# First cross-attention of a decoder layer: context split sooner, all turned blocks copied by VectorE, repeated products on TensorE, low halves of two row tiles sooner

## The chip, the cores and the metric

The kernel runs on 1 core of one Trainium2 chip. The metric is the device time of one execution in microseconds (us); lower is better. The inputs are float32 and the whole layer is one launch.

## The reference

One pre-norm decoder layer without a norm scale: self-attention, cross-attention to a context, and a gated feed-forward part with low-rank experts. Shapes: `x` is (32, 100, 512), the context (32, 361, 128), of which the causal mask lets only the first 100 rows count.

```python
def _L0_xattn_ref(q, latent_kv, Wq, Wkv_expand, Wout):
    B, S, H, NH, L = (2, 512, 512, 16, 128)
    HD = H // NH
    qp = q @ Wq.T
    kv = latent_kv @ Wkv_expand.T
    k, v = jnp.split(kv, 2, axis=-1)
    # qh, kh, vh: (b, NH, s, HD)
    scores = jnp.einsum('bhqd,bhkd->bhqk', qh, kh) * inv_sqrt_d
    causal = jnp.tril(jnp.ones((sq, sk), dtype=bool))
    scores = jnp.where(causal, scores, jnp.finfo(scores.dtype).min)
    attn = jax.nn.softmax(scores, axis=-1)
    out = jnp.einsum('bhqk,bhkd->bhqd', attn, vh)
    return out @ Wout.T

x = x + _L0_attn_ref(_layernorm(x), ...)     # 16 heads of 128, RMS-normed q and k
x = x + _L0_xattn_ref(_layernorm(x), ctx_512, ...)   # 16 heads of 32
x = x + _L0_ffn_ref(_layernorm(x), ...)      # 1408 wide, 8 experts, 2 chosen
```

## The kernel before

The layer runs in two phases. **Phase A** is self-attention over all 32 batches, in 128 steps `n` (4 groups of 4 heads by 32 batches, `STEPS` = 128). Each engine has its own loop over `n` and goes ahead by semaphores alone: in step `n` TensorE makes the scores of step `n+1`, projects what later steps need, and mixes the values of step `n-1`; ScalarE takes the exponentials of `n+1`; VectorE takes maxima, sums and low halves. Products are made in three float16 matrix multiplications (high by high, high by low, low by high; `three`, lines 1561 to 1563), so most tensors are split into a high half by ScalarE and a low half by VectorE.

**Phase B** handles the batches in groups of 5 (500 rows in 4 tiles of 125), group 0 first: cross-attention, then the feed-forward part. From group 1 on, each cross-attention is interleaved with the last product of the group before (`some_out`: three multiplications per piece, into bank 7 of the eight PSUM banks). Group 0 has no group before it (`last_nb` is 0), so nothing is interleaved there.

The start of group 0 is woven into the last steps of phase A by `begin_cross(n)` on each engine: at `B_KEYS` (126) ScalarE and VectorE split the context (`context_hi`, `context_lo`), TensorE turns two row tiles and projects three of the four key chunks (`keys`); at 127 the fourth; at 128 the values, at 129 the queries. TensorE runs `begin_cross(126)` ahead of the mixing of step 125. Weight pieces of phase B are loaded by SyncE one step ahead and split in phase A as well; the last of those (piece 13, at step 126) is split by ScalarE at line 817 and by VectorE at line 1107, each in program order with the rest of its step.

Then `cross_attention(0, 5, 0)` loops over `b` = 0 to 5. In round `b` TensorE writes the causal mask (L1832, 4 multiplications, each after the exponentials that last read its bank) and adds the scores of batch `b` (L1838, 32 small ones), turns the four probability blocks `i` of batch `b-1` (L1854, 4 each, into banks 4 and 5 in turn, after GpSimd normalized them), and mixes the values of batch `b-1` (`mix`, L1810). Somebody must copy the four turned blocks out of PSUM first: ScalarE copies 0 and 3 (L973), VectorE 1 and 2 (L1368). ScalarE takes the exponentials of batch `b`, 16 instructions of one head each (L982), VectorE the maxima before them (L1359) and the reciprocals of the sums after them (L1380); `split_b_hi` and `split_b_lo` split the last three weight pieces beside it. `mix` waits on two counters, `pTe` and `pTd`.

After round 5, VectorE adds the output projection to the rows (`add_residual`, L1384 and the statistics behind it), normalizes them (`norm`, L1227), TensorE turns the rows (`turn_row`, L1654), ScalarE takes their high halves (`row_hi`, L886) and VectorE the low halves (`row_lo`, L1232). Three of the four row tiles are "early": `route` (L1561 to 1563 with 8 columns) and `factors` for these run before the fourth tile's.

## Time and profile before

| what | value |
|---|---|
| median of 3 runs | 2577.39 us (2575.33 to 2578.66) |
| the profiled execution | 2567.62 us |
| its span | 2565.8 us |
| TensorE busy | 2458.2 us, 96% |
| VectorE, ScalarE, GpSimd busy | 1553.2, 1339.9, 843.8 us |
| mean granted TensorE clock | 0.982 of full |

The span runs from the first to the last instruction of the profiled execution; that execution's own time is 1.8 us longer than its span. PE is TensorE, DVE VectorE, ACT ScalarE, POOL GpSimd, SP SyncE. PEclk is the share of the full TensorE clock (2.4 GHz) that was granted, so 0.50 is 1.2 GHz. Phase B's first group begins near 1249 us of the span (turning of the first rows), its cross-attention loop at 1287 us, and its feed-forward part at 1367 us.

### The profile page before, as it was taken

How to read it: one execution, taken by the hardware profiler on the slowest of the kernel's cores; microseconds unless marked ns; L12 is line 12 of the kernel's file. 1: busy time of each engine (PE TensorE's matmuls, PEld its weight loads, DVE VectorE, ACT ScalarE, POOL GpSimd, SP SyncE). 2: the span in 40 equal slices, each digit the busy share in tenths (PEclk: the TensorE clock that was granted, in tenths of full speed). 3: DMA queues.
4: the chain of work that ended last, by engine and by line, in shares of the span. 5: the costliest groups of instructions: out<-in, count | busy, mean ns of one | idle time of the engine just before them, and what ended most of it. 6: DMA issues, size and time to landing. Idle time of an engine off the chain costs nothing.

```text
span 2565.8 us, 47726 instructions
## 1 busy us (share of the span) xinstructions
PE 2458.2 (96%) x16474; PEld 1333.3 (52%) x16474; DVE 1553.2 (61%) x3592; ACT 1339.9 (52%) x4109; POOL 843.8 (33%) x794
## 2 busy tenths in 40 slices
PE   6998999999999999999889999999999999999998
PEld 3554555554555555444454465465465465465466
DVE  7786766666666666666555745644645645655644
ACT  4554555555555555555454554554554563564533
POOL 3333333333333333333222422422422422422412
PEclk9999999999999999999979999999999999999999
DMA  6786667777677767797611001001001001001000
GB/s 157 149 180 161 152 151 162 167 161 169 138 170 162 168 144 190 157 195 171 139 59 57 30 13 53 5 14 54 1 18 54 1 18 54 1 18 41 7 17 14
DMA packets 456281, 241.79 MB, mean 94 GB/s; under 512 B 389136, under 2 KB 391824, under 8 KB 455284
## 3 DMA queue, kind: packets, MB, share of 16 engines
q1 hardware_dynamic: 456034, 238.63, 39.8%
q8 instruction: 139, 2.28, 0.4%
q14 instruction: 108, 0.88, 0.1%
HBM read 78.66 MB, written 32.77 MB: 43 GB/s over the span
## 4 chain that ended last, share of the span: by engine, by line
PE 89%; DVE 4%; ACT 3%; issue 3%; POOL 1%; DVEq 0%; POOLq 0%; ACTq 0%
PE ps L1561 24%; PE ps L1562 24%; PE ps L1563 24%; PE ps L1740 3%; PE ps L1741 2%; PE ps L1742 2%; PE ps L1854 2%; ACT mem L982 2%; PE ps L1838 1%; PE ps L1810 1%; PE ps L1750 1%; PE ps L1754 1%; PE ps L1752 1%; PE ps L1832 1%; PE ps L1579 1%
## 5 line engine op out<-in xcount | busy, mean ns | idle before, releaser
L1561 PE MATMUL ps<-mem 128*128 128x512 f16 (+7 forms) x3992 | 1227.9, 326 | 47.7 <-issue 31.4
L1562 PE MATMUL ps<-mem 128*128 128x512 f16 (+7 forms) x3992 | 1239.5, 326 | 0.0
L1563 PE MATMUL ps<-mem 128*128 128x512 f16 (+7 forms) x3992 | 1223.0, 325 | 0.0
L1561 PEld LDWEIGHTS ps<-mem 128*128 128x128 f16 (+3 forms) x3992 | 413.6, 104 | 374.6 <-issue 52.8
L1563 PEld LDWEIGHTS ps<-mem 128*128 128x128 f16 (+3 forms) x3992 | 414.7, 104 | 316.5 <-issue 8.6
L1562 PEld LDWEIGHTS ps<-mem 128*128 128x128 f16 (+3 forms) x3992 | 416.4, 104 | 304.8 <-issue 8.0
L757 POOL TENSOR_TENSOR mem<-mem 128x500 f32<-128x500 f32 (+1 forms) x231 | 268.7, 1164 | 470.3 <-ACT mem L1058 289.7
L707 POOL TENSOR_TENSOR mem<-mem 128x8 f32<-128x8 f32 x100 | 163.7, 1637 | 507.4 <-DVE mem L1145 507.4
L852 ACT ACTIVATE mem<-ps,mem 100x100 f32<-100x100 f32 x512 | 169.1, 346 | 186.4 <-DVE mem L1175 185.5
L1513 DVE TENSOR_TENSOR mem<-mem 128x500 f16<-128x500 f32 (+1 forms) x231 | 144.5, 649 | 171.3 <-ACT mem L1040 167.4
L719 POOL TENSOR_TENSOR mem<-mem 100x400 f16<-100x400 f32 x128 | 158.7, 1239 | 182.7 <-ACT mem L862 182.7
L832 ACT ACTIVATE mem<-ps 128x512 f32<-128x512 f32 x200 | 117.7, 589 | 168.8 <-DVE mem L1139 86.1
L771 POOL TENSOR_TENSOR mem<-mem 100x400 f32<-100x400 f32 x128 | 107.5, 852 | 290.5 <-DVE mem L1380 290.4
L1040 ACT ACTIVATE mem<-mem 128x500 f16<-128x500 f32 (+1 forms) x231 | 127.9, 585 | 111.7 <-POOL mem L757 111.3
L1206 DVE SCALAR_TENSOR_TENSOR mem<-ps,mem 128x512 f32<-128x512 f32 x100 | 69.0, 690 | 174.7 <-PE ps L1563 174.6
L982 ACT ACTIVATE mem<-ps,mem 100x100 f32<-100x100 f32 x512 | 168.5, 379 | 8.2 <-DVE mem L1359 8.2
L842 ACT ACTIVATE mem<-ps,mem 128x128 f16<-128x128 f32 x400 | 113.9, 368 | 83.7 <-POOL mem L707 83.7
L1139 DVE TENSOR_REDUCE mem<-mem 128x4 f32<-128x512 f32 x200 | 136.2, 681 | 31.8 <-ACT mem L832 31.8
L1524 DVE TENSOR_TENSOR mem<-ps,mem 128x500 f32<-128x500 f32 (+1 forms) x154 | 97.3, 632 | 66.9 <-PE ps L1563 66.6
L713 POOL TENSOR_TENSOR mem<-mem 100x400 f32<-100x400 f32 x128 | 109.1, 852 | 73.0 <-DVE mem L1185 73.0
L1153 DVE SCALAR_TENSOR_TENSOR mem<-ps,mem 128x128 f32<-128x128 f32 x400 | 112.1, 343 | 34.3 <-POOL mem L707 34.2
L982 ACT ACTIVATION_READ_ACCUMULATOR mem<-ps,mem 100x1 f32 x512 | 124.9, 244 | 0.0
(123 smaller groups left out, 3043.9 us busy)
## 6 DMA issues: line engine op xcount, KB each, us to landing
x<-mem SPq DMA_DIRECT2D x100, 256.0 KB, 2.8
mem<-x SPq DMA_DIRECT2D x75, 256.0 KB, 3.6
mem<-in_x SPq DMA_DIRECT2D x50, 256.0 KB, 3.5
mem<-x SPq DMA_DIRECT2D x12, 1000.0 KB
mem<-mem SPq DMA_DIRECT2D x32, 200.0 KB
mem<-mem SPq DMA_DIRECT2D x6, 1000.0 KB
out<-mem SPq DMA_DIRECT2D x6, 1000.0 KB
mem<-in_wq SPq DMA_DIRECT2D x16, 256.0 KB, 4.2
```

Source lines behind the costliest of these rows:

```text
L707: pool.tensor_tensor(rr[:, u % 2, :], ms[:, u % 2, :], half[:, 0:2 * HG], ALU.pow).then_inc(s["rr"], 1)
L719: pool.tensor_tensor(p_split[0:S, n % 2, 1, :, 0:S], probs[0:S, :, :], p_split[0:S, n % 2, 0, :, 0:S], ALU.subtract).then_inc(s["plo"], 1)
L757: pool.tensor_tensor(hh[:, i, 0:gs], gate[:, i, 0:gs], ub[:, 0:gs] if i == 0 else up[:, i - 1, 0:gs], ALU.mult).then_inc(c["h"], 1)
L832: act.activation(sq[:, :, :], bank(kind, u).rearrange("p (h d) -> p h d", d=D), ACT.Square).then_inc(s["sq" + kind], 1)
L852: op = act.activation(probs[0:S, h, :], ps_s[0:S, h * S:(h + 1) * S], ACT.Exp, bias=mx[0:S, h:h + 1], accum_out=den[0:S, h:h + 1])
L982: op = act.activation(cprobs[0:S, i, m, :], ps[0:S, i, m * S:(m + 1) * S], ACT.Exp, bias=cmx[0:S, i, m:m + 1], accum_out=cden[0:S, i, m:m ...
L1040: act.activation(hb_hi[:, jj, 0:gs] if i == 0 else hs_hi[:, i - 1, 0:gs], hh[:, i, 0:gs], ACT.Copy).then_inc(c["hhi"], 1)
L1139: dve.tensor_reduce(ss[:, i, m * HG:(m + 1) * HG], sq[:, :, :], AX.X, ALU.add).then_inc(s["ss"], 1)
L1513: dve.tensor_tensor(lo, hh[:, i, 0:gs], hi, ALU.subtract).then_inc(c["hlo"], 1)
L1561: pe.matmul(out_ap, ah, bh, start=(i == 0), stop=False)
L1562: pe.matmul(out_ap, ah, bl, start=False, stop=False)
L1563: mm = pe.matmul(out_ap, al, bh, start=False, stop=(i == len(pairs) - 1))
```

## The change

Four edits, all for group 0 alone.

1. The context is split one step sooner: `context_hi` and `context_lo` move from step 126 to step 125 (`B_CONTEXT`). ScalarE now waits there for the last transposing DMA of self-attention (`qkT`), whose space the split context takes. On ScalarE the two `row_hi` of step 126 move ahead of that step's exponentials, on VectorE the two `row_lo` ahead of that step's `inverse_sum`.
2. VectorE copies all four turned blocks in rounds 1 to 4; ScalarE still copies 0 and 3 in round 5. The copies stand between VectorE's maxima and reciprocals, and the low half of a weight piece goes behind the reciprocals.
3. TensorE repeats products of 512 columns (`repeat`) into bank 7, which nobody reads: 2 ahead of each of three mask blocks, 2 ahead of turning block 2, 4 ahead of `mix`.
4. After round 5, `row_lo` of tiles 0 and 1 stands ahead of `add_residual` of tile 3.

```diff
+        B_CONTEXT = STEPS - 3
 # ScalarE
             def begin_cross(n):
+                if n == B_CONTEXT:
+                    act.wait_ge(s["qlo"], ALL)
+                    act.wait_ge(s[f"qkT{(ALL - 1) % 2}"], turned(ALL - 1))
+                    context_hi(0, GS)
                 if n == B_KEYS:
-                    act.wait_ge(s["qlo"], ALL)
-                    context_hi(0, GS)
                     for t in range(2):
                         row_hi(0, t, TM, t)
...
                 for u in turned_tile(n):
                     rows_hi(u)
+                if n <= B_KEYS:
+                    begin_cross(n)
                 if 0 <= n + 1 < STEPS:
                     exponentials(n + 1)
...
-                if n == B_KEYS:
-                    begin_cross(n)
...
                 for b in range(nb + 1):
-                    if b:
+                    if b and (last_nb or b == nb):
                         take_turned(b - 1, 0)
                     if b < nb:
                         exponentials(b, 0)
                         exponentials(b, 1)
-                    if b:
+                    if b and (last_nb or b == nb):
                         take_turned(b - 1, 3)
 # VectorE
                 if n == B_KEYS:
-                    context_lo(0, GS)
-                    for t in range(2):
-                        row_lo(0, t, TM, t)
                     for m in range(3):
                         take_ck(0, GS, m)
...
                     take_o_lo(n - 2)
+                if n == B_CONTEXT:
+                    context_lo(0, GS)
+                if n == B_KEYS:
+                    for t in range(2):
+                        row_lo(0, t, TM, t)
...
-                                    ).then_inc(c["pTd"], 1)
+                                    ).then_inc(c["pTe" if i in (0, 3) else "pTd"], 1)
...
                         for i in range(4):
                             largest_scores(b, i)
-                            if b and i >= 2:
+                            if b and i and not last_nb:
+                                take_turned(b - 1, i - 1)
+                            if b and i >= 2 and last_nb:
                                 take_turned(b - 1, i - 1)
...
+                        for i in range(4):
+                            invert_sum(b, i)
+                            if b and i == 0 and not last_nb:
+                                take_turned(b - 1, 3)
                         for n in (beside_first(b - 1) if b and not last_nb else []):
                             split_b_lo(n)
-                        for i in range(4):
-                            invert_sum(b, i)
...
+                ahead = 0 if last_nb else 2
+                for t in range(ahead):
+                    row_lo(g * 2 * NT + nt, t, tm, t)
                 for t in range(len(early), nt):
                     add_residual(t)
                 first = len(early) if not last_nb else min(2, len(early))
-                for t in range(first):
+                for t in range(ahead, first):
                     row_lo(g * 2 * NT + nt, t, tm, t)
 # TensorE
+                def repeat(n):
+
+                    for _ in range(0 if last_nb else n):
+                        pe.matmul(ps[:, 7, :], cwo_hi[:, 0, 0:P], cwo_hi[:, 1, :], start=True, stop=True)
...
                             if b:
+                                if i:
+                                    repeat(2)
                                 pe.wait_ge(c["exp"], g * 4 * GB + 4 * (b - 1) + i + 1)
...
                         if b:
+                            if b < nb and i == 2:
+                                repeat(2)
                             pe.wait_ge(c["norm"], g * 4 * GB + 4 * (b - 1) + i + 1)
...
                     if b:
+                        if b < nb:
+                            repeat(4)
                         mix(b)
```

ScalarE at steps 125 and 126 of self-attention, before. L852 are the exponentials, L897 is `context_hi`, L886 `row_hi`, L817 the high half of weight piece 13, L879 `take_o_hi`.

```order
L852 ACTIVATE mem<-ps,mem 100x100 x4
L869 ACTIVATE mem<-ps 128x512
L862 ACTIVATE mem<-mem 100x4x100
L879 ACTIVATE mem<-ps 128x4x100
L852 ACTIVATE mem<-ps,mem 100x100 x4
L862 ACTIVATE mem<-mem 100x4x100
L897 ACTIVATE mem<-mem 128x500
L886 ACTIVATE mem<-ps 128x4x125 x2
L817 ACTIVATE mem<-mem 128x1408
L879 ACTIVATE mem<-ps 128x4x100
```

The same stretch after the change, in which the lines are L853, L898, L887, L818 and L880.

```order
L898 ACTIVATE mem<-mem 128x500
L853 ACTIVATE mem<-ps,mem 100x100 x4
L870 ACTIVATE mem<-ps 128x512
L863 ACTIVATE mem<-mem 100x4x100
L880 ACTIVATE mem<-ps 128x4x100
L887 ACTIVATE mem<-ps 128x4x125 x2
L853 ACTIVATE mem<-ps,mem 100x100 x4
L863 ACTIVATE mem<-mem 100x4x100
L818 ACTIVATE mem<-mem 128x1408
L880 ACTIVATE mem<-ps 128x4x100
```

The split of the context and of the rows went ahead of exponentials; the weight piece stays ahead of the `take_o_hi` that follows it.

VectorE in round 1 of the cross-attention loop, before (L1359 maxima, L1368 copies of turned blocks, L1107 a weight piece, L1380 reciprocals, L1351 `take_o`).

```order
L1359 TENSOR_REDUCE mem<-ps 100x4 x3
L1368 COPY mem<-ps 100x400
L1359 TENSOR_REDUCE mem<-ps 100x4
L1368 COPY mem<-ps 100x400
L1107 SCALAR_TENSOR_TENSOR mem<-mem 128x1408
L1380 RECIPROCAL mem<-mem 100x4 x4
L1351 TENSOR_TENSOR mem<-ps,mem 128x4x100
```

After (L1364 maxima, L1373 copies, L1385 reciprocals, L1110 the weight piece, L1356 `take_o`).

```order
L1364 TENSOR_REDUCE mem<-ps 100x4 x2
L1373 COPY mem<-ps 100x400
L1364 TENSOR_REDUCE mem<-ps 100x4
L1373 COPY mem<-ps 100x400
L1364 TENSOR_REDUCE mem<-ps 100x4
L1373 COPY mem<-ps 100x400
L1385 RECIPROCAL mem<-mem 100x4
L1373 COPY mem<-ps 100x400
L1385 RECIPROCAL mem<-mem 100x4 x3
L1110 SCALAR_TENSOR_TENSOR mem<-mem 128x1408
L1356 TENSOR_TENSOR mem<-ps,mem 128x4x100
```

Two copies more, one of them between the second and third maximum, and the weight piece behind all reciprocals.

TensorE from the turning of a round to the scores of the next, before (L1854 turning, L1810 `mix`, L1832 masks, L1838 scores).

```order
L1854 MATMUL ps<-mem 100x100 x16
L1810 MATMUL ps<-mem 32x100 x16
L1832 MATMUL ps<-mem 100x400 x4
L1838 MATMUL ps<-mem 100x100 x16
```

After (L1875, L1827, L1851, L1857; L1815 is `repeat`).

```order
L1875 MATMUL ps<-mem 100x100 x8
L1815 MATMUL ps<-mem 128x512 x2
L1875 MATMUL ps<-mem 100x100 x8
L1815 MATMUL ps<-mem 128x512 x4
L1827 MATMUL ps<-mem 32x100 x16
L1851 MATMUL ps<-mem 100x400
L1815 MATMUL ps<-mem 128x512 x2
L1851 MATMUL ps<-mem 100x400
L1815 MATMUL ps<-mem 128x512 x2
L1851 MATMUL ps<-mem 100x400
L1815 MATMUL ps<-mem 128x512 x2
L1851 MATMUL ps<-mem 100x400
L1857 MATMUL ps<-mem 100x100 x16
```

Twelve repeated products stand in each such stretch; the first one (scores of batch 0 to those of batch 1) has only the six among the masks.

## Rows read from the trace of the kernel before

**Rows 1.** Busy us (x instructions) per engine by stretch; last: granted clock, DMA share, GB/s.

```profile
1256.00:1259.50 3.50, 3.44 (x9) 1.34 (x10) 2.50 (x4) 1.38 (x1) 0.00 (x0) 0.50 0.45 120
1297.00:1315.50 18.50, 15.87 (x173) 11.29 (x169) 11.15 (x24) 15.64 (x73) 6.65 (x8) 0.50 0.35 109
1351.80:1358.50 6.70, 6.68 (x46) 5.22 (x47) 0.42 (x1) 0.00 (x0) 0.00 (x0) 0.50 0.32 131
1494.00:1534.00 40.00, 39.99 (x427) 27.73 (x426) 22.57 (x59) 26.96 (x142) 14.36 (x18) 1.00 0.01 2
...
1554.00:1554.50 0.50, 0.50 (x3) 0.15 (x1) 0.43 (x3) 0.00 (x0) 0.00 (x0) 0.50 1.04 303
```

**Rows 2.** Timeline of TensorE around the first keys: start, us, what, idle before.

```profile
1248.95 1.03 PE L1654 MATMUL ps<-mem 125*128 125x125 f32 x8
1256.06 0.58 PE L1561 MATMUL ps<-mem 128*128 128x500 f16 x1 [6.08 <-issue]
...
1264.37 0.20 PE L1561 MATMUL ps<-mem 100*128 100x100 f16 x1
```

**Rows 3.** Timeline of ScalarE in the same stretch.

```profile
1246.50 0.35 ACT L852 ACTIVATE mem<-ps,mem 100x100 f32<-100x100 f32 x1 [2.39 <-DVE mem L1175]
...
1257.24 1.38 ACT L817 ACTIVATE mem<-mem 128x1408 f16<-128x1408 f32 x1 [1.38 <-DMA mem<-in_wu]
```

**Rows 4.** Timeline of VectorE in the same stretch.

```profile
1254.95 1.01 DVE L1248 SCALAR_TENSOR_TENSOR mem<-mem 128x500 f16<-128x500 f32 x1 [2.04 <-ACT mem L897]
...
1260.52 1.62 DVE L1107 SCALAR_TENSOR_TENSOR mem<-mem 128x1408 f16<-128x1408 f32 x1
1263.05 0.69 DVE L1206 SCALAR_TENSOR_TENSOR mem<-ps,mem 128x512 f32<-128x512 f32 x1 [0.92 <-PE ps L1563]
1263.66 0.56 DVE L1190 SCALAR_TENSOR_TENSOR mem<-ps,mem 128x400 f16<-128x400 f32 x1
```

**Rows 5.** Chain of waits: exponentials of batch 0, and round 2 of the loop.

```profile
1289.55 5.34 ACT mem L982 x32
...
1306.33 0.85 PE ps L1854 x4
...
1310.77 1.56 PE ps L1810 x32
1312.33 1.62 PE ps L1832 x4
1313.95 1.60 PE ps L1838 x32
```

**Rows 6.** Timeline of TensorE, group 1's loop: the same steps at full clock.

```profile
1499.84 0.38 PE L1742 MATMUL ps<-mem 128*125 128x512 f16 x1
1500.05 0.84 PE L1832 MATMUL ps<-mem 100*100 100x400 bf16 x4
1500.82 0.96 PE L1838 MATMUL ps<-mem 32*100 32x100 f32 x32
...
1501.72 0.47 PE L1854 MATMUL ps<-mem 100*100 100x100 f32 x3
```

**Rows 7.** Timeline of VectorE, group 0, round 2: maxima, then one copy.

```profile
1306.35 1.54 DVE L1359 TENSOR_REDUCE mem<-ps 100x4 f32<-100x400 f32 x3
1307.87 0.57 DVE L1368 COPY mem<-ps 100x400 f32<-100x400 f32 x1
```

**Rows 8.** Timeline of TensorE: turning in round 4, output projection of tiles 0 and 1.

```profile
1324.70 3.21 PE L1854 MATMUL ps<-mem 100*100 100x100 f32 x16
...
1332.07 0.63 PE L1561 MATMUL ps<-mem 128*125 128x512 f16 x1
...
1335.99 0.51 PE L1854 MATMUL ps<-mem 100*100 100x100 f32 x4
```

**Rows 9.** Timeline behind the loop: low halves, first `route` product.

```profile
1349.93 1.84 DVE L1232 TENSOR_TENSOR mem<-ps,mem 128x500 f16<-128x500 f32 x3
...
1351.82 0.27 PE L1561 MATMUL ps<-mem 128*125 128x8 f16 x1 [3.25 <-DVE mem L1232]
```

## The prediction

> **What bounds the kernel now.** I read the shares of busy time first: TensorE is busy 96% of the span, so time can only be won where it waits or runs at half clock. The busy time and granted clock by stretch show where: the change touches group 0 alone, and there the cross-attention loop runs at a clock of 0.50 from 1297.0 to 1315.5, while the same loop of group 1, with multiplications of 512 columns between its parts, runs at 1.00 [rows 1]. TensorE's timeline then shows three places in group 0 that end in waits: 6.08 us idle before the first keys [rows 2], the rounds of the loop, and 3.25 us idle before `route` [rows 9]. The chain of waits says what a round is made of [rows 5].
>
> **Head: the context sooner.** At 1249.98 TensorE has turned its two row tiles and stands until 1256.06. What ends last is VectorE's `context_lo` (1254.95 plus 1.01), behind ScalarE's `context_hi` [rows 2, 4]. One step earlier ScalarE waits 2.39 us for a maximum anyway [rows 3], and the new wait on the transposing DMA is one that the scores of step 126 have too, so `context_hi` costs nothing there; `context_lo` falls into a wait of VectorE on those exponentials. If it did not, its 1.01 us would delay the reciprocals. The keys can then start at about 1250.0, and the two `row_hi` put ahead of the last exponentials delay them by no more than their own 1 us, on a path that has 4.9 us to spare (below).
>
> Not all 6 us are won, since the next wait stands close behind. The mixing of step 126 (1264.37 [rows 2]) needs the output of step 125 copied and split. On ScalarE that copy stands behind weight piece 13, which starts when its DMA lands, at 1257.24, and that DMA is not moved [rows 3]. So ScalarE is free near 1258.5 and has copied at 1259.0; VectorE, from 1258.7, does its half of the piece (1.62), a sum (0.69), and the low half (0.56) [rows 4]: 1258.7 + 2.87 = 1261.5. TensorE gets through the keys, a mixing, an output projection, the fourth keys and two turned tiles by about 1256.6 and stands for 4.9 us. The gain is 1264.4 - 1261.5 = 2.9 us. From it goes the clock: after 6.08 us idle TensorE ran its next 3.4 us at 0.50 [rows 1], a loss of 1.7 that lies inside the 14.4 us compared. After 4.9 us idle I expect half clock again, now behind the mixing, and take 1.2 of the 1.7, as part of the slow time may lie in the idle time. **Head: 1.7 us**, from 0.2 (the piece's DMA lands a little later, full loss) to 2.9.
>
> **The loop.** Before, the third round starts turning at 1306.33 and the fifth at 1324.70 [rows 5, 8]: 9.2 us a round. The chain in it [rows 5]: first turned block 0.85, ScalarE's copy, two sets of exponentials (16 take 5.34, so 8 take 2.7), its other copy, `mix` 1.56, masks 1.62, scores 1.60; what is left of 9.2 for the two copies is 0.9. `mix` waits for ScalarE's second copy, and all TensorE's parts are at half clock.
>
> After, I count from the end of the scores, at full clock. Masks cost 0.77 there and scores 0.90 (starts in group 1 [rows 6]); a turned block is 0.35 (group 1, half of 0.85 and a bit less), `mix` 0.82, half of 1.56 and a bit. A repeated product takes 0.215, as one of 512 columns from start to start there [rows 6]; half clock doubles it. VectorE: a maximum each 0.49, a copy each 0.49 with 0.57 to its end [rows 7]. It runs maximum 0 to 0.55, 1 to 1.0, copy 0 to 1.6, maximum 2 to 2.0, copy 1 to 2.6, maximum 3 to 3.0, copy 2 to 3.5, a reciprocal, copy 3 to 4.2. TensorE turns blocks 0 and 1 by 0.7, repeats two (1.1), turns 2 at 1.6 and 3 at 2.6 behind the copies that free their banks, repeats four (3.8), waits until 4.2 and mixes until 5.0. ScalarE, now without copies, has its four sets of exponentials done at 0.65 + 5.15 = 5.8. Masks with six repeated products: 5.0 + 0.77 + 1.3 = 7.06, past the last exponentials at 5.8; scores to **8.0 us**. So the repeated products themselves now bound the round; VectorE is close behind, since its weight piece (1.6) and `take_o` (0.57) come after the last reciprocal: 5.9 + 2.1 = 8.0. ScalarE ends near 7.5. Group 1's rounds, with 18 such products, also take 8.0.
>
> That gives 3 rounds at 9.2 - 8.0 = 3.6 us. The first stretch (batch 0 to batch 1) is bound by exponentials either way and wins only the clock of its last mask and the scores, 0.2 + 0.65 = 0.85. The last: output projection of tile 0 started 7.4 after the scores (1332.07 against 1324.70 [rows 8]) and can start once the exponentials end, 5.85, so 1.5; its 12 products took 3.9 us of which half lay at half clock, against 2.6 [rows 8], 1.3 more. Sum 7.3. The clock may still fall: in the first stretch TensorE stands for a maximum and the first exponentials, 2 us, and then has short pieces between exponentials. I take off 1.0 for that, an estimate between nothing and about 2 (one stretch of 3.4 us at half, as in the head). **Loop: 6.3 us.**
>
> Moved with it: piece 16's DMA is issued only after the low half of piece 14, now 3 us later in its round; ScalarE needs it after the next exponentials, one round of 8 later, and I count at most 0.5 us, within the rounding.
>
> **Tail.** `route` waits for three low halves in a row (1.84 [rows 9]) behind the fourth tile's statistics. Two of them now run during the projection: the wait shrinks by 2 x 0.6 = 1.2 us, to some 2.0. TensorE then ran 6.7 us at 0.50 [rows 1], worth 3.3 us. Part may come back. But in group 1 the clock was also 0.50 just after `route` with no idle at all before it [rows 1], so 8-column products do not hold the clock here. I take 1.0, between 0 and 3.2. **Tail: 2.2 us.**
>
> **Sum.** 1.7 + 6.3 + 2.2 = 10.2 us. Against the profiled execution's 2567.62 that is 2557.4; against the median, 9.8 above it, 2577.4 - 10.2 = **2567.2 us**. About 0.2% (5.2 us) is what a measurement of this kernel can tell from no change. All of TensorE's work behind the tail is dense, so nothing gives the time back.
>
> **Rivals.**
>
> *A. The clock swings.* The twelve products leave three gaps of about 0.5 us in a round, and the first stretch has longer ones. For it: the clock was 0.50 there with TensorE busy 15.87 of 18.5 us [rows 1], so being busy alone did not raise it. Against it: group 1 holds 1.00, but with 18 products and no gaps. If every round spends one stretch of about 3 us at half, it costs 1.2 to 1.7 more; the loop gains 2 and the whole is 6: 2571.5. The Trainium skill, TensorE: Matmul & The Clock Gate, section A second HAM failure mode: psum-queue depth-cycling, speaks for this rival: small idles between groups of matmuls, it says, let the clock go back and forth. By that rule the loop comes out as in this rival; no row here shows a loop with such gaps and such products.
>
> *B. Slower: repeated products at half clock.* If they don't raise the clock, each is 0.43 us, and they stand on TensorE's own path: turning and the first two 2.56, the rest of the turning 4.25, four more 5.96, `mix` 7.5, masks with six more 11.7, scores 13.3 us a round. Three rounds lose 4.0 each and the last 1.4: 13.4, less head and tail 3.9, 9.5 slower: 2587. It decides from where more than about two of the rounds stay at half. Against it: the first keys, dense products of 500 columns, brought the clock up within 3.5 us [rows 1], and at half clock the rounds would be dense.
>
> *C. VectorE takes over.* It makes two copies more a round, holds back maxima 2 and 3, and has its weight piece behind the last reciprocal. If its order costs 1 us a round, rounds are 9.0: the loop wins 3.3 and the whole about 7 or, with a late piece 16, 3: 2573. The sum above is nearly tied, which speaks for it; group 1, where VectorE has no pieces, says nothing.
>
> *D. More than forecast.* Full clock kept in head, loop and tail: 2.9 + 7.3 + 4.4 = 14.6: 2562.8.
>
> **Numbers.** Forecast 0.50, A 0.20, B 0.05, C 0.10, D 0.15. The range 2561.5 to 2573.5 takes in D, A and C with a run's own spread, and leaves out B and the far end of C. Faster by over 0.2% (below 2572.2): forecast, D, most of A: 0.84. Same: C and the rest of A: 0.11. Slower: B, 0.05.
>
> **What would show it.** In the profile after: keys at about 1250 with no idle ahead; a wait of some 5 us now ahead of the mixing of step 126, behind ScalarE's weight piece at 1257; rounds of 8.0 us with a granted clock near 1.00 and no copy on ScalarE in them; output projection 5.9 us after the last scores; two low halves ahead of the fourth tile's sum and a wait of about 2 us before `route`. A clock of 0.5 to 0.7 in the rounds says A, a round over 11 us says B, a TensorE waiting for VectorE's first maximum or copy with a clock of 1.00 says C. I would be wrong in kind if the loop gained nothing at full clock.

## The result, and the profile after

The changed kernel takes 2570.52 us (median of 20 runs, 2561.25 to 2574.64). The kernel before, run beside it, takes 2574.78 us (20 runs, 2564.77 to 2579.11). The ratio is 0.9984 with a 95% interval of 0.9977 to 0.9992: 4.1 us faster, between 2.1 and 5.9. The forecast was a gain of 10.2 us.

The profiled execution took 2572.42 us, its span 2570.6 us. Its first 1256 us (self-attention) are 7.1 us longer than in the profile before; five more profiles with the same code there have it at 1248.3 to 1255.4, so this is scatter and every comparison below is counted from the turning of the first two row tiles: 1248.95 before, 1256.07 after.

The page's first part, engine by engine; VectorE has 8 instructions more than in the kernel before, which had 3592, and ScalarE 8 fewer (4109):

```profile
PE 2468.0 (96%) x16522; PEld 1331.6 (52%) x16522; DVE 1557.5 (61%) x3600; ACT 1336.8 (52%) x4101; POOL 847.0 (33%) x794
```

Busy time by stretch after, columns as in [rows 1]. In order: the wait ahead of the mixing of step 126, what follows it, the first stretch of the loop, its rounds, the tail:

```profile
1263.80:1268.80 5.00, 0.04 (x2) 0.04 (x2) 2.86 (x4) 2.72 (x4) 0.00 (x0) 0.88 0.62 123
1268.80:1274.40 5.60, 5.60 (x23) 2.56 (x24) 1.60 (x3) 0.50 (x1) 0.00 (x0) 0.50 0.30 97
1295.00:1299.00 4.00, 1.91 (x37) 1.08 (x35) 2.44 (x6) 2.29 (x15) 0.59 (x1) 0.91 0.43 123
1303.00:1327.60 24.60, 21.53 (x306) 13.21 (x299) 19.07 (x42) 20.09 (x103) 13.58 (x13) 1.00 0.27 83
1351.70:1358.50 6.80, 6.74 (x49) 4.80 (x50) 0.55 (x2) 0.00 (x0) 0.04 (x1) 0.59 0.32 126
```

The rounds, at 0.50 before, run at 1.00. The stretch behind the mixing is at 0.50 for 5.6 us, and the tail is slow as before.

**Head.** TensorE's timeline, answering to [rows 2], then ScalarE's and VectorE's, answering to [rows 3, 4]:

```profile
1256.07 1.03 PE L1666 MATMUL ps<-mem 125*128 125x125 f32 x8
1256.94 0.38 PE L1573 MATMUL ps<-mem 128*128 128x500 f16 x1
...
1268.79 0.24 PE L1573 MATMUL ps<-mem 100*128 100x100 f16 x1 [4.96 <-DVE mem L1193]
```

```profile
1264.53 1.38 ACT L818 ACTIVATE mem<-mem 128x1408 f16<-128x1408 f32 x1 [2.81 <-DMA mem<-in_wu]
```

```profile
1265.94 1.63 DVE L1110 SCALAR_TENSOR_TENSOR mem<-mem 128x1408 f16<-128x1408 f32 x1 [3.99 <-ACT mem L818]
1267.48 0.69 DVE L1209 SCALAR_TENSOR_TENSOR mem<-ps,mem 128x512 f32<-128x512 f32 x1
1268.08 0.57 DVE L1193 SCALAR_TENSOR_TENSOR mem<-ps,mem 128x400 f16<-128x400 f32 x1
```

The keys start with no idle. The mixing of step 126 waits 4.96 us behind weight piece 13, whose DMA landed 8.5 us after the turning, as before (8.3). It starts 12.72 us after the turning instead of 15.42: 2.7 sooner. But the half clock behind it costs what it won: the first mask of the loop starts 38.28 us after the turning, against 38.24. The granted clock was at 0.50 for 6.8 us both times, from 1252.8 to 1259.6 before and from 1267.6 to 1274.4 after. Before, 3.3 us of that fell into the wait, where they cost nothing, and 3.5 behind it; after, 1.2 fell into the wait and 5.6 behind it.

**Loop.** The chain of waits through round 2, answering to [rows 5]:

```profile
1310.44 1.02 PE ps L1857 x32
...
1314.65 0.86 PE ps L1815 x4
1315.51 0.03 issue
1315.54 0.89 PE ps L1827 x32
1316.44 0.30 PE ps L1851
1316.74 0.43 PE ps L1815 x2
1317.17 0.17 PE ps L1851
1317.34 0.43 PE ps L1815 x2
1317.78 0.17 PE ps L1851
1317.95 0.43 PE ps L1815 x2
1318.38 0.17 PE ps L1851
1318.56 0.89 PE ps L1857 x32
```

From scores to scores the rounds take 7.99, 8.11 and 8.19 us, against 9.22 each before. In the last round TensorE waits for a copy, because the low halves of weight piece 16 (the last, in two parts) stand ahead of VectorE's maxima. VectorE's timeline, then TensorE's:

```profile
1325.65 0.18 DVE L1385 RECIPROCAL mem<-mem 100x4 f32<-100x4 f32 x1 [1.13 <-ACT mem L985]
1325.74 2.32 DVE L1110 SCALAR_TENSOR_TENSOR mem<-mem 128x1152 f16<-128x1152 f32 x2
```

```profile
1330.14 0.52 PE L1875 MATMUL ps<-mem 100*100 100x100 f32 x4 [1.23 <-DVE mem L1373]
```

**Tail.** The wait ahead of `route` is 2.08 us instead of 3.25 [rows 9]:

```profile
1351.76 0.22 PE L1573 MATMUL ps<-mem 128*125 128x8 f16 x1 [2.08 <-DVE mem L1235]
```

Together, group 0 from the turning to the first product of its feed-forward part (`turn_mask`, the turning of the router's result) takes 110.84 us instead of 117.93. That is 7.1 us won. Behind it 4.8 are lost again: from there to the end of the span it is 1203.7 us, against 1198.9.

**Where it is given back.** The feed-forward part of each group begins when VectorE has worked out the router's choice, a chain of 11 small instructions, and TensorE waits for it at the start of `turn_mask`. Groups 1 to 4 are one loop (`Fori(1, FULL - 1)`); 0, 5 and 6 are written out. VectorE's jump back stands close ahead of this chain, which thus belongs to the iterations that the jump enters (groups 2, 3, 4). In these three, and in no other group, VectorE stops once in this chain with nothing to wait for that the profile shows ("issue"). VectorE before, group 2; of the chain's 11 instructions the tenth and the last:

```profile
1748.68 0.19 DVE L1464 TENSOR_REDUCE mem<-mem 125x4 f32<-125x32 f32 x1
1752.52 0.19 DVE L1465 TENSOR_TENSOR mem<-mem 125x32 f32<-125x32 f32 x1 [3.65 <-issue]
1752.75 0.77 DVE L1455 COPY mem<-mem 125x512 f32<-125x512 f32 x2
```

VectorE after, group 2: the third, the fourth, and the copy behind the eleventh:

```profile
1745.97 0.19 DVE L1473 SCALAR_TENSOR_TENSOR mem<-mem 125x32 f32<-125x32 f32 x1
1750.85 0.19 DVE L1476 TENSOR_REDUCE mem<-mem 125x4 f32<-125x32 f32 x1 [4.69 <-issue]
...
1752.66 0.77 DVE L1467 COPY mem<-mem 125x512 f32<-125x512 f32 x2
```

The stop stands ahead of the last link (the eleventh) before, ahead of the fourth after. So 8 links of 0.227 us follow it instead of 1, and by this TensorE waits 7 x 0.227 = 1.6 us longer, in each of three groups: an estimate of 4.8 us. TensorE's waits there, before (group 2 at full clock, group 3 after 3.4 us at half):

```profile
1753.23 0.43 PE L1921 MATMUL ps<-mem 125*128 125x125 f32 x2 [1.96 <-DVE mem L1455]
...
1948.54 0.65 PE L1921 MATMUL ps<-mem 125*128 125x125 f32 x4 [0.29 <-DVE mem L1455]
```

After, group 2 behind such a stretch at half clock:

```profile
1753.15 1.07 PE L1944 MATMUL ps<-mem 125*128 125x125 f32 x8 [1.86 <-DVE mem L1467]
```

and in a second profile of the changed kernel, group 2 at full clock:

```profile
1747.24 1.93 PE L1944 MATMUL ps<-mem 125*128 125x125 f32 x8 [3.72 <-DVE mem L1467]
1748.96 0.62 PE L1573 MATMUL ps<-mem 128*128 128x500 f16 x1
```

Like with like, 0.29 became 1.86 and 1.96 became 3.72. And after the 3.72 the clock is at half (eight turnings take 1.93 us, not 1.07), which costs more.

That the estimate equals the 4.8 us of this pair of profiles is chance. From the `turn_mask` of group 1 to that of group 4, the three iterations with the stop, it is 585.7 us after and 582.6 before, 3.2 more. The step to group 5, which has no stop, is 3.3 us longer, and the one from group 0 to group 1 is 1.7 shorter; both differ by stretches at half clock. Over all profiles below, the three iterations take 581.3 to 582.6 us where the stop is ahead of link 11 (4 profiles, mean 582.2) and 585.7 to 589.0 where it is ahead of link 4 (10 profiles, mean 587.8). The place of the stop is thus worth about 5.6 us, of which 4.8 are the links by the estimate; the rest goes with stretches at half clock.

### The profile page after: what moved, and what is told of

It is laid out like the page before. It is cut to its first block, busy times and chain, and to the rows that moved or that the text cites. A ratio compares the mean times of both kernels' runs of the same rounds, so it can differ in the third digit from the quotient of the medians.

```text
span 2570.6 us, 47822 instructions
## 1 busy us (share of the span) xinstructions
PE 2468.0 (96%) x16522; PEld 1331.6 (52%) x16522; DVE 1557.5 (61%) x3600; ACT 1336.8 (52%) x4101; POOL 847.0 (33%) x794
## 4 chain that ended last, share of the span: by engine, by line
PE 88%; DVE 5%; ACT 3%; issue 3%; POOL 1%; DMA 0%; SPq 0%; DVEq 0%; POOLq 0%; ACTq 0%
PE ps L1573 24%; PE ps L1574 24%; PE ps L1575 24%; PE ps L1752 3%; PE ps L1753 2%; PE ps L1754 2%; PE ps L1875 2%; ACT mem L985 2%; PE ps L1857 1%; PE ps L1827 1%; PE ps L1762 1%; PE ps L1766 1%; PE ps L1764 1%; PE ps L1851 1%; PE ps L1591 1%
## 5 line engine op out<-in xcount | busy, mean ns | idle before, releaser
L1574 PEld LDWEIGHTS ps<-mem 128*128 128x128 f16 (+3 forms) x3992 | 417.5, 105 | 306.7 <-issue 11.4
L853 ACT ACTIVATE mem<-ps,mem 100x100 f32<-100x100 f32 x512 | 169.1, 346 | 186.0 <-DVE mem L1178 185.9
L1752 PE MATMUL ps<-mem 128*125 128x512 f16 (+1 forms) x312 | 121.3, 389 | 3.2 <-DVE mem L1339 1.9
```

What stands on the lines that cost most here:

```text
L853: op = act.activation(probs[0:S, h, :], ps_s[0:S, h * S:(h + 1) * S], ACT.Exp, bias=mx[0:S, h:h + 1], accum_out=den[0:S, h:h + 1])
L1574: pe.matmul(out_ap, ah, bl, start=False, stop=False)
L1752: pe.matmul(ps[0:tm, 7, :], h_hi, w_hi, start=(j == 0), stop=False)
```

## The experiments

Apart from the two repeats, each is an edit of the changed kernel; the kernel before was timed beside it. The table shows, for one profile each, the start of the mixing of step 126 and of the first mask (us after the turning of the first two row tiles), the scores of batch 1 to 2, 2 to 3 and 3 to 4, the time from `route` to `turn_mask`, and group 0 in all; then before which link of the router chain VectorE stops in groups 2 to 4, the time from the `turn_mask` of group 1 to that of group 4 ("three iterations"), and the time from the `turn_mask` of group 0 to the end of the span. Of `route` to `turn_mask`, 15.1 us have 6.8 at half clock in them and 13.5 us have 3.4. A ratio of 0.0010 below 1 is 2.6 us; gains below are worked out from the ratio.

| kernel | mixing | first mask | rounds | route to turn_mask | group 0 | stop before link | three iterations | group 0 to end | ratio to before (95%) |
|---|---|---|---|---|---|---|---|---|---|
| before | 15.42 | 38.24 | 9.22 9.22 9.22 | 15.06 | 117.93 | 11 | 582.6 | 1198.9 | |
| before again | 15.79 | 38.61 | 9.22 9.23 9.22 | 15.09 | 118.52 | 11 | 581.3 | 1199.3 | 0.9999 (0.9989 to 1.0009) |
| changed | 12.72 | 38.28 | 7.99 8.11 8.19 | 15.15 | 110.84 | 4 | 585.7 | 1203.7 | 0.9984 (0.9977 to 0.9992) |
| changed again | 12.49 | 38.26 | 7.99 8.11 8.21 | 15.16 | 110.85 | 4 | 588.7 | 1204.3 | 0.9984 (0.9974 to 0.9994) |
| no head | 15.29 | 38.11 | 8.69 8.11 8.20 | 13.55 | 109.98 | 4 | 587.2 | 1206.8 | 0.9992 (0.9981 to 1.0003) |
| piece later | 11.80 | 36.11 | 8.85 8.26 8.20 | 13.53 | 108.27 | 4 | 589.0 | 1206.7 | 0.9988 (0.9977 to 0.9998) |
| no repeats | 12.48 | 37.78 | 8.87 8.88 8.75 | 15.12 | 113.87 | 4 | 587.3 | 1206.9 | 1.0007 (0.9997 to 1.0016) |
| scalar copies | 11.33 | 35.83 | 8.77 8.50 8.60 | 15.14 | 111.23 | 11 | 582.4 | 1200.4 | 0.9972 (0.9959 to 0.9985) |
| piece last | 7.65 | 30.47 | 8.13 8.10 8.21 | 13.53 | 101.76 | 4 | 589.0 | 1206.6 | 0.9970 (0.9958 to 0.9981) |
| fill first | 12.01 | 37.79 | 7.98 8.11 8.20 | 13.54 | 110.43 | 4 | 588.5 | 1204.4 | 0.9982 (0.9972 to 0.9992) |
| tail repeats | 12.75 | 38.38 | 7.98 8.12 8.20 | 11.87 | 107.66 | 4 | 585.7 | 1204.0 | 0.9992 (0.9983 to 1.0002) |
| all | 7.69 | 30.52 | 7.98 8.11 8.20 | 13.55 | 102.37 | 4 | 588.5 | 1204.5 | 0.9955 (0.9942 to 0.9968) |
| all, scalar copies | 7.63 | 30.45 | 7.98 8.50 8.60 | 11.87 | 100.39 | 11 | 582.6 | 1203.9 | 0.9909 (0.9894 to 0.9924) |
| all, fewer | 7.67 | 30.49 | 7.34 8.11 9.68 | 11.89 | 99.83 | 4 | 588.6 | 1208.1 | 0.9945 (0.9925 to 0.9965) |

**Without the head's edits.** Context and rows are split where they were before.

```diff
-                if n == B_CONTEXT:
+                if n == B_KEYS:
                     act.wait_ge(s["qlo"], ALL)
-                    act.wait_ge(s[f"qkT{(ALL - 1) % 2}"], turned(ALL - 1))
                     context_hi(0, GS)
...
-                if n <= B_KEYS:
-                    begin_cross(n)
...
+                if n == B_KEYS:
+                    begin_cross(n)
...
                 if n == B_KEYS:
+                    context_lo(0, GS)
+                    for t in range(2):
+                        row_lo(0, t, TM, t)
```

> The changed kernel with the head edit undone: the context is split at step 126 again, everything else as changed. Measured from the scores of step 126 to the first mask of the loop, the kernel before took 42.5 us and the changed one 42.5 us. Theory (the earlier keys are paid back, because the idle stands later and the clock stays at 0.50 for 5.6 us of work behind it instead of 3.4): 42 to 43 us again, and a total within 1 us of the changed kernel. Rival (the head edit is worth 2 to 3 us and the one profile of the changed kernel was unlucky): again 42.5 here, but the other runs of this call that keep the head edit take 40 to 41, and this one is 2 to 3 us slower than they.

2572.31 us. Its first mask comes at 38.11, with the head's edits at 38.28: **in group 0 the head edit wins nothing**, though the mixing is 2.6 us sooner with it. That is what the expectation called theory.

**The piece split a step later, its load unmoved.**

```diff
-            return [k for k, at in enumerate(B_SPLIT) if at == n]
+            return [k for k, at in enumerate(B_SPLIT) if at + (k == 13) == n]
```

> The changed kernel with weight piece 13 split one step later (127 instead of 126) on ScalarE and VectorE, its DMA where it was. Theory (the head's gain ends on that piece, which stands ahead of the copy of step 125's output): TensorE no longer idles 4.96 us ahead of the mixing of step 126, the granted clock stays at 1.00, and scores of step 126 to first mask takes 34 to 36 us instead of 42.5; the whole is 6 to 9 us faster than the changed kernel. Rival (something else holds the mixing of step 126 or 127 back, a transposing DMA of the probabilities or the values' copies): an idle of 3 us or more remains with another releaser, and 40 us or more.

2569.61 us. The mixing did not start when VectorE's half was free; it now waits for a DMA, as the rival had it. SyncE's issues and TensorE's timeline of this kernel:

```profile
1254.23 0.57 SPq L543 DMA_DIRECT2D mem<-in_wu  x1
1254.90 1.26 SPq L611 DMA_TRANSPOSE mem<-mem  x1
```

```profile
1264.44 0.24 PE L1573 MATMUL ps<-mem 100*128 100x100 f16 x1 [3.89 <-DMA mem<-mem]
```

The DMA that transposes the probabilities of step 126 was issued 0.7 us behind the load of the piece and took until 1264.44, 9.5 us. The piece thus held the mixing in two ways, it seems, and the split was only the one that ended last; the next run tests it.

**The piece loaded and split three steps later.** It moves the load behind the transposing DMA.

```diff
-            return [k for k, at in enumerate(B_SPLIT) if at == n]
+            return [k for k, at in enumerate(B_SPLIT) if at + 3 * (k == 13) == n]
...
-            return [k for k, at in enumerate(B_SPLIT) if at - 1 == n]
+            return [k for k, at in enumerate(B_SPLIT) if at - 1 + 2 * (k == 13) == n]
```

> The changed kernel with weight piece 13 both loaded two steps later (behind the transposing DMA of step 126's and 127's probabilities) and split three steps later. With only the split moved, the mixing of step 126 waited for its transposing DMA, issued 0.7 us behind the piece's load and landing 9.5 us after its issue. Theory (that DMA lands late because it stands behind the piece's 704 KB, and this is the last wait of the head): the mixing of step 126 starts about 6.5 to 7.5 us after the turning of the first two row tiles instead of 12.7, the clock stays at 1.00 and turning to first mask takes 29.5 to 31 us instead of 38.3; the whole is 6 to 9 us faster than the changed kernel. Rival (a transposing DMA takes over 9 us here whatever stands before it): the wait remains, 36 us or more, and no gain over the changed kernel beyond 2 us.

2563.94 us. The mixing follows its predecessor without idle, in TensorE's timeline:

```profile
1263.76 1.02 PE L1666 MATMUL ps<-mem 125*128 125x125 f32 x8
1264.86 0.20 PE L1573 MATMUL ps<-mem 100*128 100x100 f16 x1
```

It starts 7.65 us after the turning, there is no half clock behind it, and the first mask comes at 30.47: 7.8 us sooner than in the changed kernel, 5.1 at the mixing and 2.8 by the clock. With the load behind it, the transposing DMA was not waited for at all.

**No repeated products** (`for _ in range(0)` in `repeat`; nothing that is read is left out).

> The changed kernel without any repeated product; its outputs are the same, as nobody reads them. Theory (they are what lifts the clock in the loop): the clock is near 0.5 to 0.7 in the loop and a round takes 8.5 to 9.2 us, so the loop (first mask to turning in round 4) is 2 to 4 us longer than the 33.2 us of the changed kernel. Rival (VectorE's copies alone shorten the rounds, repeats only cost): rounds of 7.0 to 7.5 at a clock near 1.00, and the loop 2 to 3 us shorter.

2575.18 us. Rounds of 8.87, at half clock where the changed kernel is at 1.00; the stretch from the exponentials of batch 0 into the third round, columns as in [rows 1]:

```profile
1296.00:1305.00 9.00, 6.54 (x51) 4.30 (x51) 4.01 (x11) 7.10 (x38) 3.06 (x4) 0.50 0.31 119
1305.00:1320.00 15.00, 13.38 (x161) 9.68 (x160) 10.51 (x23) 11.64 (x56) 9.23 (x8) 0.53 0.37 116
```

So the products do hold the clock, and that is worth 0.6 to 0.9 us a round; the copies' new place is worth some 0.35 (9.22 to 8.87).

**ScalarE copies blocks 0 and 3 again, repeated products stay.** ScalarE's `take_turned` is taken in every round, VectorE's `take_turned(b - 1, 3)` and those of block 0 go.

> The changed kernel with turned blocks 0 and 3 copied by ScalarE again in all rounds; repeated products stay. Theory (with the clock at 1.00 the round is bound by TensorE's own row of products and by exponentials, so who copies hardly matters): rounds of 7.7 to 8.1 us against 8.1 now, total within 1.5 us of the changed kernel. Rival (VectorE's copies are what takes 9.2 down): rounds of 8.8 us or more, and 2 to 3 us slower.

2565.82 us, 7.2 us below before (3.9 to 10.6). In group 0 the rounds are 0.4 to 0.8 longer than in the changed kernel, nearer to the rival's 8.8 than to the theory's 7.7 to 8.1; the 8.77 has 1.8 us at half clock in it. Yet the kernel isn't slower than the changed one, which is 4.1 below before (2.1 to 5.9), and neither expectation had that; the two intervals overlap, so that it is faster isn't shown by this run alone. Its VectorE has 3592 instructions again, its router chain stops before link 11, and the three iterations take 582.4 us, as before.

**Nine products ahead of the first mask of batch 1, four ahead of its others.**

```diff
-                                if i:
-                                    repeat(2)
+                                if i or b == 1:
+                                    repeat((4 if i else 9) if b == 1 else 2)
```

> The changed kernel with more repeated products in the first stretch of the loop: 9 ahead of the first mask of batch 1 and 4 instead of 2 ahead of each of the other three, all inside waits for exponentials. In four of five profiles so far the clock fell to 0.50 in that stretch for 3.4 or 6.8 us. Theory (it falls because TensorE stands 2 us and then waits between short pieces): the clock stays at 1.00 and the scores of batch 2 begin 16.0 us after the first mask, as in the best profile, not 17.0; 0.8 to 1.2 us won against the usual case, nothing lost. Rival (the clock falls there anyway, or the added products hold up the masks): 17 us or more.

2567.04 us, ratio 0.9982. The clock no longer falls in the loop's first stretch, yet the scores of batch 1 come as late after the first mask as in the changed kernel (8.05 us against 8.04). In both, each of the four masks starts as ScalarE has finished a set of four exponentials, 1.30 us apart, so a faster TensorE wins nothing there.

**Nine products ahead of the first `route`.**

```diff
+                    repeat(9)
                     route(0, len(early))
```

> The changed kernel with 9 repeated products ahead of the first route product, in the 2.08 us that TensorE waits there. Changed kernel: 15.15 us from the first route product to the feed-forward part with 6.8 us at 0.50 there, or 13.2 to 13.5 with 3.4 us. Theory (the waiting lets the clock fall, and the 8-column products behind it do not bring it back): with the wait filled at most 3.4 us at half clock, 13.2 us or less, some 11.7 if none. Rival (the 8-column products alone cost the clock, as in group 1): 13.2 to 15.2 as before, and no difference in total.

2568.68 us, ratio 0.9992. In the profile the tail is 3.3 us shorter (11.87 against 15.15) with the granted clock at 1.00:

```profile
1345.00:1352.00 7.00, 6.86 (x67) 4.84 (x65) 1.13 (x2) 0.00 (x0) 0.55 (x1) 1.00 0.31 121
```

The median doesn't show it: the gain is 2.1 us (4.4 at most, and nothing isn't ruled out). The groups behind cost what they cost in the changed kernel (1204.0 us to the end), so this run leaves 3 us open.

**The piece three steps later and both sets of added products together**, and VectorE's half of a piece ahead of the last three reciprocals instead of behind them. The last edit:

```diff
                                 take_turned(b - 1, 3)
-                        for n in (beside_first(b - 1) if b and not last_nb else []):
-                            split_b_lo(n)
+                                for n in beside_first(b - 1):
+                                    split_b_lo(n)
```

> The last three together, and VectorE's low halves of pieces 14 to 16 ahead of the last three reciprocals instead of behind them, so that they no longer hold back the next maxima (piece 16 did by 1.2 us). If the terms add up: head 7 to 9 us, first stretch 1, fourth round 0.8 to 1, tail 1 to 3 less than the changed kernel, in all 10 to 13 us below it, so near 2558 to 2560 us. If the gains are paid back by the clock elsewhere, as half of the first change's were: 5 us or less.

2560.10 us, 11.6 us below before (8.2 to 14.9), where the expectation's sum had put it. Group 0 has 102.37 us, 8.5 less than in the changed kernel, and the head gives 7.8 of them. The wait for a copy after the scores of batch 4 fell from 1.23 to 0.44 us. But the clock was at 0.50 for 3.4 us behind the loop and for 3.4 behind `route`: nine products ahead of `route` did not hold it this time (13.55 us, where the other three kernels with them have 11.87, 11.87 and 11.89).

**The changed kernel and the one before once more**, unaltered.

> The changed kernel once more, unaltered: a second profile of group 0 and more runs. In the first pair of profiles the change won 7.1 us from the turning of the first two row tiles to the feed-forward part (117.9 to 110.8), in the medians 4.1. Theory (the changed kernel's profile was a lucky one in the loop, where the clock did not lose more than a microsecond, and the stretches at half clock differ from run to run by 1.7 us each): 110.8 to 113.5 us now, and a ratio near 0.998 again. Rival (the change costs something outside group 0): again 110 to 111, with the ratio as it was.

> The kernel before once more, unaltered, for a second profile of the same stretch: 117.9 us the first time. If the stretches at half clock fall as differently here, 116 to 119.5; its total should agree with the kernel before within 0.1%.

2568.78 us, 0.9984 (0.9974 to 0.9994), and 2573.27 us, 0.9999. The first result repeats: group 0 again takes 110.85 us, so its profile was not a lucky one, and from there to the end of the span it is 1204.3 us against 1199.3, 5.0 us given back. Here the three iterations alone are 7.5 us longer, and the others 2.4 shorter.

**All, with ScalarE's copies.** The kernel with all edits together, but with blocks 0 and 3 on ScalarE. It sets the two theories against each other: in group 0 VectorE's copies are better, in the loop over groups 1 to 4 VectorE's eight instructions more are worse.

> The four edits of the fastest version so far, with blocks 0 and 3 copied by ScalarE in all rounds. With the changed kernel as base this swap made rounds of 8.5 to 8.8 us instead of 8.1 in the profile, but its runs were 4.7 us below the changed kernel's. Theory (the copies on VectorE are worth 0.3 to 0.5 us a round, and that gap in the totals was scatter): 1 to 2 us slower than the version with VectorE's copies (2560.1), rounds 8.4 to 8.8. Rival (ScalarE's copies are better in a way that the stretch does not show): 2 to 4 us faster than it.

2551.48 us (6 runs, 2549.57 to 2562.17), against 2573.14 for the kernel before: **0.9909 (0.9894 to 0.9924), 23.4 us faster (19.6 to 27.3), the best version** (the medians lie 21.7 apart). It is 8.6 us below its twin with VectorE's copies, more than even the rival had expected, and the intervals of the two don't overlap. The rounds are 7.98, 8.50 and 8.60. The stop is where it was before, in VectorE's timeline of group 2:

```profile
1743.90 0.19 DVE L1474 TENSOR_TENSOR mem<-mem 125x32 f32<-125x32 f32 x1 [3.63 <-issue]
```

The three iterations take 582.6 us, as before, and 5.9 less than in the twin. The profile is of this kernel's slowest run, 10 us above the others. In it group 0 wins 17.5 us, self-attention is 7.1 longer than in the profile before, and from group 0 to the end it takes 1203.9 us, with more stretches at half clock ahead of the first iteration with a stop and behind the last. So where the rest of the gain beyond 17.5 us comes from no trace shows.

**All, with one product where there were two** (ahead of masks from batch 2 on; VectorE's copies).

> The same four edits, with one repeated product instead of two ahead of three masks in the rounds of batches 2 to 4. Theory (at full clock TensorE's own row bounds the round): a round is 0.65 us shorter, about 7.4 to 7.5 instead of 8.1 to 8.2, and the loop 2 us, at a clock still at 1.00. Rival (VectorE's next maxima bound it already, or the clock falls with fewer products): rounds of 8.0 us or more.

2560.63 us, 0.9945 (0.9925 to 0.9965): the rounds come out as 7.34, 8.11 and 9.68, in sum 0.8 us more than with two products. The theory holds for the first. In the second TensorE waits 1.22 us for VectorE's copies: VectorE's maxima stand behind its copy of the mixed values (`take_o`), and that waited 1.48 us for ScalarE, which has a weight piece to split. In the third the clock was at 0.50 for 3.4 us behind such a wait of 1.30 us. The ratio doesn't differ from that with two products by more than the intervals.

## Why the prediction was right in kind and wrong in size

The time, 2570.52 us, lies in the range and the kernel is faster. The gain does not have the size forecast: 4.1 us (2.1 to 5.9), of 10.2. Against the 2577.39 that the prediction started from it is 6.9 us, but 2.6 of those are the kernel before, which ran at 2574.78 beside it. Started from 2574.78, the range would have ended at 2570.9, so that the time lies in it owes something to luck. At 0.16% the gain also falls below the 0.2% that the prediction called the least that can be told from no change, so beside the runs of before it is the case that had a chance of 0.11; with 20 runs the interval still excludes no gain at all. The parts that the prediction summed came to 7.1 us of its 10.2 in group 0: the head 0 of 1.7, the loop with the tail's wait 7.2 of 7.5, the tail's clock 0 of 1.0. The rest was lost behind group 0.

- **The keys at once, then the wait behind piece 13:** right. The mixing was to wait 4.9 us and did wait 4.96; it was to gain 2.9 us and gained 2.7.
- **The clock behind it, 1.2 us:** wrong in size. TensorE ran 5.6 us at 0.50 after this wait, a loss of 2.8 (half of 5.6), where 3.4 us were expected. The head is worth 0, as the kernel without its edits confirms. The forecast took the 3.4 us behind the wait of before for the whole stretch and expected part of it to fall into the new wait. The stretch was 6.8 us long both times, and a smaller part of it fell into the new wait, which is shorter: 1.2 us instead of 3.3.
- **Rounds of 8.0 at full clock:** right, 8.0 to 8.2; three rounds gained 3.4 of 3.6. The repeated products hold the clock, against rival B and, in the rounds, against rival A. The Trainium skill, TensorE: Matmul & The Clock Gate, section A second HAM failure mode: psum-queue depth-cycling, says that small idles between groups of matmuls let the clock go back and forth; with two gaps of 0.44 to 0.65 us in each round this loop stayed at 1.00 for 24.6 us, so here it did not come true. In the loop's first stretch the clock did fall, for 3.4 us behind a wait of 2.09.
- **The last round:** part of rival C. "At most 0.5 us" for the late piece was wrong: the late DMA did no harm, but the piece's 2.32 us on VectorE stand ahead of the maxima and TensorE waits 1.23 us there. The output projection starts 6.8 us after the last scores, where 5.9 were forecast. First mask to `route` was to shrink by 6.3 us plus the 1.2 of the tail's wait, and shrank by 7.2. (Rival C's own numbers with a late piece 16, 3 us off 2577.4, give 2574.4 and not its 2573.)
- **The tail:** the wait shrank by 1.2 us as forecast. The 1.0 taken for the clock was 0; `route` to `turn_mask` is 15.15 us, against 15.06. It can be had, though not each time: with nine products ahead three profiles have 11.9 us and one 13.55.
- **"All of TensorE's work behind the tail is dense, so nothing gives the time back":** this step failed. It took the mean share of 96% for the groups behind, and did not look at TensorE's wait ahead of each `turn_mask` (1.96 us in group 2), where VectorE decides. Behind group 0, 4.8 us of 7.1 were lost in the first pair of profiles and 5.0 in the second. The moved stop, worth about 5.6 us in the three iterations over all profiles, accounts for that; the rest is scatter of the clock.

Group 0's gain against 117.93, less 3 x 1.6 us for a stop before link 4, can be held against the gain by the ratio:

| kernel | by this sum | measured (95%) |
|---|---|---|
| changed | 2.3 | 4.1 (2.1 to 5.9) |
| no head | 3.2 | 2.1 (-0.8 to 4.9) |
| piece later | 4.9 | 3.1 (0.5 to 5.9) |
| no repeats | -0.7 | -1.8 (-4.1 to 0.8) |
| scalar copies | 6.7 | 7.2 (3.9 to 10.6) |
| piece last | 11.4 | 7.7 (4.9 to 10.8) |
| fill first | 2.7 | 4.6 (2.1 to 7.2) |
| tail repeats | 5.5 | 2.1 (-0.5 to 4.4) |
| all | 10.8 | 11.6 (8.2 to 14.9) |
| all, scalar copies | 17.5 | 23.4 (19.6 to 27.3) |
| all, fewer | 13.3 | 14.2 (9.0 to 19.3) |

Eight of eleven lie inside their interval. Piece last and tail repeats come out 3 to 4 us worse than the sum, and all with scalar copies 6 better. TensorE's clock behind the waits in groups 1 to 4 varies from run to run by pieces of 1.7 us (half of 3.4), and there is one profile of each, so this remains open.

**What the stop is.** No edit was made for it alone, but the traces tell much. In all 14 profiles VectorE has from 1480 us on exactly one such stop in each of the three iterations entered by a jump, and none in a group entered straight (one profile, without the head's edits, has a second pause of 3.06 us put down to "issue" in group 2; it is the one right behind the jump, 2.8 to 3.5 us from the jump to the next row, which every profile has and which elsewhere ends with TensorE's result). The stop is before link 11 in all four profiles of kernels whose VectorE has 3592 instructions (two of before, two with ScalarE's copies), and before link 4 in the ten whose VectorE has 3600, the eight more being copies ahead of the loop.

- *It has a fixed place.* Of all rows that VectorE has in the trace, those of its sequencer included, 3134 stand ahead of the first stop in each of the 14 profiles, 3517 ahead of the second and 3900 ahead of the third. Ahead of the first jump stand 3112 rows where VectorE has 3592 instructions and 3126 where it has 3600. So the chain moved by 14 rows, 7 links with a row of the sequencer each, and the stop did not move. ScalarE, which lost the eight copies, has no such stop.
- *It has a fixed end.* VectorE goes on 8.83 to 9.04 us after its jump in all 42 cases. Between the jump and the stop it gets through 21 rows with 3592 instructions, and through 7 with 3600.
- *Instructions are fetched then.* The trace's DMA records have one packet of 8192 bytes of the kind "instruction" that starts 7.05 to 7.30 us after the jump, in all 42 cases, and VectorE goes on 1.72 to 1.79 us after it started. After the fourth and last of these rows, where the loop is left, there is neither such a packet at that time nor a stop.

So VectorE waits for its own instructions behind the jump, and eight instructions more ahead of the loop bring the chain to the far side of that wait. The Trainium skill, Runtime: NRT & Kernel Launch, section Instruction fetch mechanics, says that instructions are fetched in blocks of 256, and that a taken branch to a block that isn't at hand makes the engine wait for a DMA. The trace agrees with the second; of the first it shows packets of 8192 bytes on this queue, half of the 16 KiB that the section gives for a block. Why the packet starts only 7 us after the jump no run shows.

## What to carry to other kernels

Instructions added in one place can cost time in a loop that the edit doesn't touch: after each run compare the engines' idle "issue" in every iteration, not just the stretch that changed, and try a second version with the engine's instruction count ahead of the loop as it was. Before pricing a shorter wait of TensorE at what it is shorter by, look at where the half clock falls: a wait of 5 us here cost 2.8 more behind it, one of 6 us 1.8. And where a wait has two causes that end within a microsecond of each other (a split, and the DMA queued behind its load), move both: the split alone won 0.9 us at the mixing, load and split 5.1.

## What the runs showed of the hardware

- In an iteration entered by a jump VectorE stood 3.3 to 5.3 us without a cause in the profile's views, behind 3134 of its rows in all 14 profiles, and went on 8.83 to 9.04 us after the jump, 1.72 to 1.79 us after an 8192-byte instruction packet had started. Eight instructions more ahead of the loop (14 rows) brought 7 links of a chain behind that place.
- A transposing DMA issued 0.7 us behind the load of a 128x1408 float32 piece took 9.5 us to release TensorE; issued ahead of the load, the one of the same step was not waited for.
- A stretch of TensorE at half clock ahead of a wait can be free: before, the wait was 0.29 us with 3.4 us at half ahead of it and 1.96 us without. Behind a wait, 3.4 us at half cost 1.7 us.
- Busy TensorE is not TensorE at full clock: without repeated products it was busy 13.38 of 15 us at 0.53, with them 21.53 of 24.6, a similar share, at 1.00. What it was busy with differed: the second had 12 products of 512 columns in each round.
